# A four-layer graph network: H of the later layers in homes of its own, and maps moved between the sums

## The reference

```python
h = jnp.maximum(_layernorm(x, axis=-1), 0.0)
def _sage_conv(x, src, dst, Wl, Wr, b):
    agg = jax.ops.segment_sum(x[src], dst, num_segments=n)
    deg = jax.ops.segment_sum(jnp.ones_like(dst, dtype=x.dtype), dst, num_segments=n)
    mean = agg / jnp.maximum(deg, 1.0)[:, None]
    return mean @ Wl + x @ Wr + b
h = relu(sage_conv(h, ..., Wl1, Wr1, b1))     # 256 -> 256
h = relu(sage_conv(h, ..., Wl2, Wr2, b2))     # 256 -> 128
h = relu(sage_conv(h, ..., Wl3, Wr3, b3))     # 128 -> 256
out = x + sage_conv(h, ..., Wl4, Wr4, b4)     # 256 -> 256
```

## Time and profile before

| | us |
|---|---|
| median of 3 runs | 731.82 (731.35 to 734.61) |
| profiled execution, whole | 732.57 |
| profiled execution, span | 730.5 |
| TensorE matmul busy in the span | 671.8 (92%) |
| VectorE busy | 292.2 (40%) |
| ScalarE busy | 172.4 (24%) |

### The profile page before, as it was taken

One profiled execution on the slowest core, in us unless ns is written; L12 is line 12 of the kernel. 1 busy time (PEld: TensorE's weight loads), 2 busy tenths in 40 slices (PEclk: granted clock), 3 DMA queues, 4 the chain that ended last, 5 costly groups with the idle time before them and its releaser, 6 DMA issues.

```text
span 730.5 us, 11548 instructions
## 1 busy us (share of the span) xinstructions
PE 671.8 (92%) x4545; PEld 366.5 (50%) x4546; DVE 292.2 (40%) x826; ACT 172.4 (24%) x339; POOL 31.1 (4%) x80
## 2 busy tenths in 40 slices
PE   5578898999999999999959999899989999999997
PEld 4234555655554555644434444444434646556464
DVE  6898866686767757601011221212221101001001
ACT  4844753363624503210101010111120000000000
POOL 7000000000000000000000000000000110110110
PEclk9999999899999999999979999999999999999999
DMA  8000012300101001064423235222346222130230
GB/s 260 18 2 1 30 61 89 108 1 6 58 17 56 13 8 58 17 14 112 132 83 106 87 106 185 81 78 87 115 138 212 81 78 63 39 102 20 80 100 29
DMA packets 39425, 53.50 MB, mean 73 GB/s; under 512 B 8558, under 2 KB 21519, under 8 KB 39377
## 3 DMA queue, kind: packets, MB, share of 16 engines
q1 hardware_dynamic: 39260, 52.59, 23.5%
q10 hardware_dynamic: 116, 0.24, 0.1%
HBM read 31.86 MB, written 20.97 MB: 72 GB/s over the span
## 4 chain that ended last, share of the span: by engine, by line
PE 84%; DVE 7%; ACT 3%; DMA 3%; issue 2%; POOL 1%; SPq 1%; DVEq 0%; POOLq 0%; ACTq 0%
PE agg_ps L1720 39%; PE window_ps L1720 12%; PE lin_ps L1643 6%; PE window_ps L1599 6%; PE lin_ps L1665 6%; PE lin_ps L1682 4%; PE lin_ps L1739 2%; DVE early L1146 2%; PE turn_ps L1707 2%; PE lin_ps L1690 2%; ACT counts L1373 1%; DMA H_d<-newH 1%; DMA W<-in_L_gnn_Wr_dram 1%; DMA H<-H_d 1%; PE degree_ps L1751 1%
## 5 line engine op out<-in xcount | busy, mean ns | idle before, releaser
L1720 PE MATMUL agg_ps<-counts,H 128*128 128x512 f16 (+2 forms) x1500 | 355.0, 374 | 2.1 <-DMA H<-H_d 2.1
L1720 PEld LDWEIGHTS agg_ps<-counts,H 128*128 128x128 f16 x1500 | 130.0, 99 | 119.1 <-issue 12.9
L1146 DVE TENSOR_TENSOR early<-early 128x512 f16<-128x512 bf16 (+2 forms) x466 | 153.6, 390 | 38.6 <-PE window_ps L1599 37.2
L1373 ACT ACTIVATE counts<-window_ps 128x400 f16<-128x400 f32 x196 | 96.3, 505 | 133.5 <-PE window_ps L1599 129.6
L1599 PEld LDWEIGHTS window_ps<-early 128*128 128x128 f16 x892 | 70.0, 100 | 112.7 <-issue 30.7
L1599 PE MATMUL window_ps<-early 128*128 128x100 f16 (+1 forms) x892 | 100.3, 223 | 24.4 <-DVE early L1146 14.3
L1720 PE MATMUL window_ps<-counts,H 128*128 (+1 forms) x600 | 96.2, 316 | 0.0
L1720 PEld LDWEIGHTS window_ps<-counts,H 128*128 128x128 f16 x600 | 45.6, 98 | 49.6 <-issue 4.1
L1200 DVE SCALAR_TENSOR_TENSOR aggT<-agg_ps,columns,rdeg 128x512 f32<-128x512 f32 (+1 forms) x30 | 20.5, 715 | 101.1 <-PE agg_ps L1720 89.8
L835 POOL TENSOR_TENSOR newH<-newH,early 128x256 f32<-128x256 f32 (+1 forms) x25 | 17.4, 725 | 680.9 <-DMA newH<-in_x_dram 680.9
L1219 DVE COPY newH<-turn_ps 128x1024 f16<-128x1024 f16 (+1 forms) x28 | 17.7, 632 | 58.6 <-PE turn_ps L1707 58.6
(11 more groups left out here) (159 smaller groups left out, 381.2 us busy)
## 6 DMA issues: line engine op xcount, KB each, us to landing
selfT<-hT_d SPq DMA_DIRECT2D x18, 512.0 KB, 4.3
hT_d<-newT SPq DMA_DIRECT2D x12, 512.0 KB, 4.2
rdeg<-rdeg_d SPq DMA_DIRECT2D x18, 256.0 KB, 4.2
counts<-in_x_dram SPq DMA_DIRECT2D x6, 512.0 KB, 8.3
hT_d<-counts SPq DMA_DIRECT2D x6, 512.0 KB, 3.2
H_d<-newH SPq DMA_DIRECT2D x12, 256.0 KB, 2.0
H<-H_d SPq DMA_DIRECT2D x12, 256.0 KB, 4.2
H_d<-newH SPq DMA_DIRECT2D x6, 512.0 KB, 2.6
```

Of the source, the lines that this page charges most:

```text
L1146: last = v.tensor_tensor(hot[:, group % GROUPS, 0:n * size].rearrange("p (r n d) -> p r n d", r=n, d=2), numbers_to[:, 0:size].rearrange(" ...
L1373: a.activation(counts[:, :, 2 * w * WIN:2 * (w + 1) * WIN].rearrange("p t (a w) -> p a t w", a=2), window_ps[:, FILL_AT[w] % 2, 0:2 * KEYS ...
L1720: last = m((agg_ps, window_ps)[bank][:, h, 0:n], H_of[:, k, part, h * P:(h + 1) * P], counts[:, k, chunk_cols(c, n)], start=first and part ...
```

## The change

- `H_tiles(l, k, n)` gives each layer's H a home: layer 1 the tensor `H`; layer 2 a part of `early` (the scratch of the building of counts, free after layer 1's place 5); layer 3 the first part of `H`; layer 4 the rest of `early` and of `H`. VectorE's `copy_turned` writes the turn straight into the next layer's home, except for layer 1, where the first six chunks still go through DRAM, as `early` is in use; six loads (`load_H`) bring them, five of them in `after(5)`.
- The weights of layer 3 move from `early` to `plan`, which becomes 128 rows high. `Wr2` gets a semaphore of its own, `wr2_loaded`. The next layer's first `selfT` and `rdeg` are loaded by `first_loads` when the last map is done.
- `FIRST_BANK`: the bank of a layer's first sums is the one that the last sums of the layer before do not use. TensorE starts a layer when all scales but the last are done, and `REST_AT` puts the last map after two tiles.
- `first_rests`: the maps and turns of the first two chunks stand among the third chunk's sums.
- The sums of the last tile take its 53 rows alone (`rows_`), since a home's other rows aren't written.

```diff
+        def H_tiles(l, a, n):
+            if l == 1:
+                return H[:, a:a + n, :, :]
+            width = 2 * (F2 if AGG[l] == 1 else D)
+            if l == 2:
+                at, home = WR2 + a * width, early
+            elif l == 3:
+                at, home = a * width, raw
+            elif a >= IN_EARLY:
+                at, home = WR2 + (a - IN_EARLY) * width, early
+            else:
+                at, home = HALF + a * width, raw
+            return home[:, at:at + n * width].rearrange("p (t h f) -> p t h f", t=n, h=2)
...
+        FIRST_BANK = [0, 0, 1, 0, 1]
-        REST_AT = {1: (0, 4, 9), 2: (0, 8), 3: (0, 7, 11)}
+        REST_AT = {1: (2, 6, 11), 2: (2, 10), 3: (2, 6, 9)}
...
+                def first_loads(l):
+                    sp.wait_ge(hT_stored[l - 1], 16 * (NCH - 1))
+                    load_self(0, l)
+                    if l == 2:
+                        sp.wait_ge(rdeg_stored, 16 * NCH)
+                        sp.dma_start(Wr2_sb, Wr2.rearrange("(k p) n -> p k n", p=P)).then_inc(wr2_loaded, 16)
+                    sp.wait_ge(agg_scaled[l - 1], AGG[l - 1] * NCH)
+                    load_rdeg(0, l)
...
                 def after(q, last=False):
                     sp.wait_ge(lin_done[l], both(q + 1, LIN[l], 1 if l == 4 else LIN[l]))
+                    if last and l < 4:
+                        first_loads(l + 1)
...
+                    if l == 1 and isinstance(q, int) and q == NCH - 2:
+                        sp.wait_ge(H_stored, 16 * (NCH - 2))
+                        for j in range(NCH - 2):
+                            load_H(j)
                     if l < 4:
                         store_new(q)
-                        store_H(q)
+                        if l == 1 and not last:
+                            store_H(q)
...
-                    sp.wait_ge(agg_done[l], AGG[l] * NCH)
-                    sp.wait_ge(H_stored[l], 16 * (NCH - 1))
-                    for c in ORDER[:-1]:
-                        sp.dma_start(H_to[:, a:b, :], H_d[l][:, a:b, :]).then_inc(H_loaded[c], 16)
...
+                if l == 1 and q < NCH - 1:
+                    if q > 0:
+                        dve.wait_ge(H_stored, 16 * q)
+                    to = newH_flat(2 * F2)[:, 0:t, :].rearrange("p t (a f) -> p t a f", a=2)
+                else:
+                    to = H_tiles(l + 1, c * TPC, t)
...
                 if l == 2 and isinstance(q, int) and q == 0:
+                    pe.wait_ge(wr2_loaded, 16)
+                if l == 3 and isinstance(q, int) and q == 0:
                     pe.wait_ge(late_loaded, LATE)
...
-                H_of = H if AGG[l] == 2 else Hn
+                rows_ = TAIL if l > 1 and k == NT - 1 else P
+                tile = H_tiles(l, k, 1)[0:rows_, 0, :, :]
...
+            def first_rests(l):
+                return {2: {2: [lambda: lin(2, 0)], 8: [lambda: turn(2, 0, 0)],
+                            13: [lambda: lin(2, 1)], 19: [lambda: turn(2, 1, 0)]},
+                        3: {2: [lambda: lin(3, 0)], 8: [lambda: turn(3, 0, 0)], 12: [lambda: turn(3, 0, 1)],
+                            15: [lambda: lin(3, 1)], 19: [lambda: turn(3, 1, 0)], 22: [lambda: turn(3, 1, 1)]},
+                        4: {2: [lambda: lin(4, 0)], 10: [lambda: lin(4, 1)]}}[l]
...
-                pe.wait_ge(agg_scaled[l - 1], AGG[l - 1] * NCH)
+                pe.wait_ge(agg_scaled[l - 1], AGG[l - 1] * (NCH - 1))
...
-                    pe.wait_ge(H_loaded[c], 16 * (l - 1))
-                    add_sources(l, 0, 0, k, i == 0, i == NT - 1)
-                over_places(pe, place)
+                    if l == 2 and j < NCH - 1:
+                        pe.wait_ge(H_loaded[j], 16)
+                    else:
+                        pe.wait_ge(turn_copied[l - 1], TURNS[l - 1] * (j + 1))
+                    add_sources(l, 0, FIRST_BANK[l], k, i == 0, i == NT - 1)
+                over_places(pe, place, FIRST_BANK[l])
```

More of the change, by code:

```diff
@@ L251, in sage_stack_kernel @@
         edge_key = part[5].bitcast(f32)
[L252 to L256, removed]
+        WR2 = 2 * 2 * F2
+        Wr2_sb = early[:, 0:WR2].bitcast(f32).rearrange("p (k n) -> p k n", k=2)
+        plan_all = sb("plan", [P, 2 * NWIN], i32)
+        plan = plan_all[0:1, :].rearrange("p (w a) -> p w a", a=2)
+        W3 = plan_all[:, 0:2 * D].bitcast(f32).rearrange("p (a n) -> p a n", a=2)
+        b4rows = plan_all[:, 2 * D:3 * D].bitcast(f32)
         heavy = sb("heavy", [1, NCH], i32)
@@ L308, in sage_stack_kernel @@
         raw = H[:, :, :, :].rearrange("p t h f -> p (t h f)")
+        HALF = NT * 2 * F2
+        IN_EARLY = min(ORDER[:4]) * TPC
+        assert WR2 + max(HALF, (NT - IN_EARLY) * 2 * D) <= early.shape[-1] and HALF + IN_EARLY * 2 * D <= NT * 2 * D
+        def H_tiles(l, a, n):
[11 more added lines that the diff above has]
+            return home[:, at:at + n * width].rearrange("p (t h f) -> p t h f", t=n, h=2)
         def in_H(tile, at, n):
@@ L455, in sage_stack_kernel @@
         degree_turned = sem("degree_turned")
+        wr2_loaded = sem("wr2_loaded")
         late_loaded = sem("late_loaded")
@@ L471, in sage_stack_kernel @@
         turn_copied = [sem(f"turn_copied_{i}") for i in L]
-        H_stored = [sem(f"H_stored_{i}") for i in L]
+        H_stored = sem("H_stored")
         narrow_done = sem("narrow_done")
         summed = sem("summed")
-        H_loaded = [sem(f"H_loaded_{i}") for i in range(NCH)]
+        H_loaded = [sem(f"H_loaded_{i}") for i in range(NCH - 1)]
         x4_loaded = sem("x4_loaded")
@@ L709, in after @@
                             load_x4(q + 1)
[L711 to L715, removed]
+                if l == 1:
+                    load_self(0)
+                else:
+                    sp.wait_ge(hT_stored[l - 1], 16 * NCH)
                 if l == 2:
-                    sp.dma_start(Wr2_sb, Wr2.rearrange("(k p) n -> p k n", p=P)).then_inc(late_loaded, 16)
                     for i, w in enumerate((Wl3, Wr3)):
@@ L1307, in place @@
                         add_out(q)
-                place(0, 0)
-                over_places(dve, place)
+                if l < 4:
+                    for q in range(NCH):
+                        place(q, (FIRST_BANK[l] + q) % 2)
+                else:
+                    place(0, FIRST_BANK[l])
+                    over_places(dve, place, FIRST_BANK[l])
         @block.scalar
@@ L1512, in place @@
                         high_part(l, q, h)
-                place(0, 0)
-                over_places(act, place)
+                place(0, FIRST_BANK[l])
+                over_places(act, place, FIRST_BANK[l])
         @block.tensor
@@ L1716, in add_sources @@
                     k = TILES[k]
-                H_of = H if AGG[l] == 2 else Hn
+                rows_ = TAIL if l > 1 and k == NT - 1 else P
+                tile = H_tiles(l, k, 1)[0:rows_, 0, :, :]
                 for h in halves or range(AGG[l]):
                     for part in range(2):
-                        last = m((agg_ps, window_ps)[bank][:, h, 0:n], H_of[:, k, part, h * P:(h + 1) * P],
-                                 counts[:, k, chunk_cols(c, n)], start=first and part == 0,
+                        last = m((agg_ps, window_ps)[bank][:, h, 0:n], tile[:, part, h * P:(h + 1) * P],
+                                 counts[0:rows_, k, chunk_cols(c, n)], start=first and part == 0,
                                  stop=final and part == 1)
@@ L1830, in place @@
                     between = rest(l, q - 1)
+                    if isinstance(q, int):
+                        between = first_rests(l) if q == 2 else {}
                     if not isinstance(q, int) or q > 1:
                         pe.wait_ge(agg_scaled[l], AGG[l] * (q - 1))
+                    else:
+                        pe.wait_ge(agg_scaled[l - 1], AGG[l - 1] * NCH)
                     for k in range(NT):
@@ L1837, in place @@
                             do()
[L1841 to L1842 removed]
+                pe.wait_ge(agg_scaled[l - 1], AGG[l - 1] * (NCH - 1))
+                tiles = [(j, k) for j, c in enumerate(ORDER) for k in range(c * TPC, min((c + 1) * TPC, NT))]
                 left = [do for _, dos in sorted(rest(l - 1, NCH - 1).items()) for do in dos]
[L1844 removed]
+                for i, (j, k) in enumerate(tiles):
                     if i in REST_AT[l - 1]:
                         left.pop(0)()
[L1847 to L1849 removed]
+                    if l == 2 and j < NCH - 1:
+                        pe.wait_ge(H_loaded[j], 16)
+                    else:
+                        pe.wait_ge(turn_copied[l - 1], TURNS[l - 1] * (j + 1))
+                    add_sources(l, 0, FIRST_BANK[l], k, i == 0, i == NT - 1)
+                over_places(pe, place, FIRST_BANK[l])
             lin(4, NCH - 1)
```

60 lines of the change are left out of this document (29 added, 31 removed).

## The result

The changed kernel took 713.79 us, median of 4 runs (712.87 to 714.77); the kernel before 733.11 in the 4 runs beside it (731.35 to 734.61). The ratio is 0.9733, 95% interval 0.9701 to 0.9766. The forecast was 713. The profiled execution has a span of 711.5 us against 730.5.

What follows compares the result with a forecast made beforehand. TensorE was taken to bound the kernel, 84% of the chain of waits. Profiled 732.57 less 23.8 at the borders plus 5.0 for 53-row matmuls gave 713.8, 713 against the runs' median; own range 710 to 716.

Steps and rivals of the forecast that it cites:

- Excess at the borders: Three layer borders on TensorE: time beyond work at unit prices, 14.1, 7.3 and 3.85 us, together 25.3.
- gross gain: Borders' 25.3 us excess less 1.5 us of waits left: 23.8 us, before the 53-row matmuls' cost.
- Banks: Layer starts: two tiles ahead of the last map cover scales of 1.37, 0.99 and 0.96 us; left 0.5, 0.1, 0.
- Maps and turns: First two chunks' maps and turns among the third's sums: waits left 0.5 in layer 2, 0.3 to 0.4 in layer 3.
- The clock: Borders: 7.4 us of the excess taken as lost clock, all returning, with granted clock 1.00 from layer 1's end.
- The added cost: Last tile's 53-row matmuls in layers 2 to 4: 21 groups at 0.24 us, 5.0 us slower.
- Wr2: Border 1-2: own semaphore and earlier loads remove the weights wait; without this cover up to 5.8 us are lost again.
- Free rows: Rival at the last tile: the 53-row matmuls cost nothing, 708 us; chance 0.18.
- The kept dip: Rival at the borders: the clock dips anyway or a load comes late, 7.4 us stay, 720.5 us; chance 0.17.

Runs made afterwards that it cites:

- bank_back: Changed kernel with first sums in bank 0 and layer starts as before; 377.8 us from layer 1's last 26 sums to the end (changed kernel 374.95), ratio 0.978.
- fill: rests_back plus 13 useless 512-column matmuls in layer 3 where TensorE would wait for the two turns; 382.8 us from layer 1's last 26 sums, ratio 0.9869.
- rests_back: Changed kernel with the first chunk's map and turn back in the short chunk; 385.7 us from layer 1's last 26 sums (changed kernel 374.95), ratio 0.9888.
- full_rows: Changed kernel with the last tile's sums over 128 rows again; 370.8 us from layer 1's last 26 sums (changed kernel 374.95), ratio 0.9673.
- before_53: Kernel before with only the last tile's sums of layers 2 to 4 cut to 53 rows; 398.9 us from layer 1's last 26 sums (before 394.3), ratio 1.008.
- rows_96: Changed kernel with 96 rows instead of 53 in the last tile's sums; 370.8 us from layer 1's last 26 sums (changed kernel 374.95), ratio 0.9671.
- wr2_late: Changed kernel with layer 2's first map waiting for all late weights again; 375.0 us from layer 1's last 26 sums (changed kernel 374.95), ratio 0.9748.
- best: Changed kernel with whole tiles everywhere in the later layers and some maps moved; 368.3 us from layer 1's last 26 sums, median 706.47, ratio 0.9644.

## Why the prediction was right

I compare stretches from start to start, with 0.216 us per sum for the last one.

- **Excess at the borders.** Border 1-2 went from 49.05 (341.81 to 390.86) to 36.83 us, border 2-3 from 38.01 to 31.80, border 3-4 from 62.81 to 59.52: 12.2, 6.2 and 3.3, 21.7 in all. The changed kernel has nine of the 53-row groups in these stretches; with 0.2 each added back the gross gain is 23.5, forecast 23.8.
- **Banks.** Left were 0.51, 0.15 and 0, forecast 0.5, 0.1 and 0, and bank_back gave the part its 2.9 us.
- **Maps and turns.** The turn in layer 2 waited 0.55, forecast 0.5. Layer 3 waited 0.1 for the second turn and not at all for the short chunk's map, where I had 0.3 to 0.4. This move is the largest part: 15.25 us on the kernel before, 10.75 when taken back.
- **The clock.** The forecast let all 7.4 us of lost clock return, and the clock is 1.00 over every stretch that had been lower. fill shows for border 2-3 that filling the idle time is enough: 1.00 over 454 to 470, against 0.79 in rests_back. For border 1-2 it is argued from the timeline alone. But the 7.4 us, all that was over beyond the idle times, are not all clock. At border 3-4, 0.6 us are over though the clock was 1.00 from 527 to 604; the row of most of that stretch, of the kernel before, stands below. At border 2-3 the forecast had 2.7 (7.3 - 4.6). The stretch from the second turn to the short chunk's map, which holds the same work, takes 3.79 us in fill, 6.72 in rests_back and 471.43 - 466.51 = 4.92 in the kernel before, where it ends with the second row below.

```profile
545.00:585.00 40.00, 37.71 (x272) 21.50 (x271) 6.13 (x10) 2.02 (x3) 2.77 (x4) 1.00 0.47 157
```

```profile
471.43 0.32 PE L1682 MATMUL lin_ps<-aggT,early 128*128 128x53 f32 x2
```

So the clock cost 2.9 in rests_back, but only 1.1 to 1.3 in the kernel before (fill has 0.2 of added cost in the stretch); that 2.9 and 2.7 are near each other is chance. The forecast of the time did not suffer, as it let the whole excess return, whatever it was. The waits left, 0.5 to 0.6, have the clock at 1.00 around them.
- **The added cost.** Forecast 21 x 0.24 = 5.0, from a change in columns and one in rows; measured 4.15 (full_rows), 4.6 (before_53) and 4.15 (rows_96). This term was 0.4 to 0.85 too large: the lower bound of 0.21 was the right price. For each of the 42 changes between 128 and 53 rows that is 0.1 us.
- **Wr2.** I named the wait for the weights as gone through a semaphore of its own and earlier loads. wr2_late shows that with the earlier loads and the new place the semaphore adds nothing; in the kernel before it would have counted, for about 3.2 us by the rows at wr2_late.
- **Rivals.** Free rows would have given 708, what full_rows has (708.11). A weight load of the sums takes 98 ns, where a matmul starts every 216: time enough, as this rival had it, but at the 53-row groups the load stood idle 0.42 us on either side. The kept dip, 720.5, didn't come: no idle over 0.55 us is left at the borders. Its price of 7.4 us was too high, as said above.

Sum on the profiles: 23.5 gross less 21 x 0.2 = 4.2 is 19.3, what the measure above shows (19.35); forecast 23.8 - 5.0 = 18.8. The gross gain was 0.3 too high and the cost 0.8 too high, which offset in part. That 713 was met within 0.8 us is in part luck as well: the runs of the kernel before beside these had a median of 733.11, and the forecast started from 731.82.

## What to carry to other kernels

Count the work of a border between stages at unit prices from the undisturbed rows, and take what is over as the gain if the waits go: that gave the gross gain to 0.3 us of 24. Do not read what is over beyond the idle times as lost clock; look at the granted clock for that. A chain across other engines belongs beside the long matmuls; beside a short chunk its wait shows (2.54 us at border 1-2 in rests_back, 0.55 in the changed kernel), and can bring a slow stretch behind it (clock 0.50 over 457 to 463 in rests_back). Trimming a tile to its valid rows saved no time here: from 128 to 96 rows the time stayed at 370.8, and at 53 and at 64 rows it cost 0.2 us for each group. Where the other operand is zero in the surplus rows, whole rows can stay, as long as they hold finite numbers: zero times those is zero. Before giving loads a semaphore of their own, look at when each of them lands: it counts only where the consumer comes before the last one.

## What the hardware showed unexpectedly

- Sums with 53 and 64 contraction rows among those with 128 cost 0.2 us per group, with 96 and 128 nothing.
- A wait of 2.54 us at border 1-2 (rests_back) left the clock at 1.00 (over 364 to 371), while at border 2-3 it was 0.50 over 457 to 463, behind waits of 1.67 and 1.36 us with 0.9 us of work between. Which of the things around them decides stays open.
- The slow stretch differs in length behind the same idles: the 14 sums behind them took 4.04 us in the kernel before and 5.62 in rests_back.
- Layer 1's stretch, with the same order on TensorE in all kernels, varied by over 4 us between profiled executions. The granted clock over 60 to 180 us was 0.97 in the shortest (best) and 0.91 in the longest (before_53).
